# Grouped attentions: the rough pass for row maxima replaced by scores kept in SBUF and shifted by GpSimd and VectorE

## The chip, the cores and the metric

One Trainium2 chip, one of its cores. The metric is the device time of one execution in microseconds (us), the median of three runs. Engines: PE is TensorE (matmuls; PEld is its weight load, which runs beside it), ACT is ScalarE, DVE is VectorE, POOL is GpSimd, SP is the engine that issues most DMAs. SBUF is the on-chip memory, PSUM the eight accumulator banks that PE writes.

## The reference, cut to what matters

The program is a stack of four blocks, each a cross attention and a feed-forward part, over x of 4 x 256 tokens x 256 features, with a context of 4 x 1601 tokens. The change touches the second and the fourth attention, the "grouped" ones: 16 query heads share 4 key/value heads, head size 128. The fourth:

```python
q = rms_norm((hidden_states @ Wq).reshape(B, S, 16, 128), q_norm_w)
k = rms_norm((encoder_hidden_states @ Wk).reshape(B, 1601, 4, 128), k_norm_w)
v = (encoder_hidden_states @ Wv).reshape(B, 1601, 4, 128)
k, v = repeat(k, 4, axis=2), repeat(v, 4, axis=2)
scores = einsum("bqhd,bkhd->bhqk", q, k) / 128 ** 0.5
probs = softmax(scores, axis=-1)
out = einsum("bhqk,bkhd->bqhd", probs, v).reshape(B, S, 2048) @ Wo
```

The second is the same with a rotation by position (rope) of q and k, and with the 256 query tokens appended to the context, so 1857 keys. The softmax subtracts each query's largest score.

## The kernel before, in words

`grouped_attention` is called twice, as a1 (with rope) and a3 (without). A **group** is one batch and one key/value head: 16 groups. A group has 4 heads x 256 queries = 1024 query columns, taken in two halves of 512; half a group is called a **unit** here. Keys come in **tiles** of 128: KT = 15 with rope, 13 without. A **turn** is one key tile against 512 query columns, so a group is 30 or 26 turns. In each turn

- PE computes the scores (`scores`, L1125, L1127, L1129: three fp32r matmuls of 512 columns, high x high, high x low, low x high) with keys on the partitions, and then, for the turn before, the product with the values (`values`, L1140: four fp32 matmuls of 129 columns, the last column being the sum of the probabilities).
- ACT takes exp of the scores out of PSUM into `probs` (`exp`, L1252), and writes the negated row maxima, `negb`, into the PSUM bank in which the scores after next will accumulate (`seed`, L1262).

Since keys lie on partitions, the row maxima must be known before the scores are. So there is a **rough pass** (`R`): for each block of 128 queries PE computes high x high scores with the queries on the partitions (L1104, two times two matmuls: 1024 keys, and the rest), DVE reduces each half (L1483), takes the smaller of the two negated maxima (L1491), POOL multiplies the identity by it (L1324), and one matmul with ones (`NB`, L1112) spreads the 512 maxima of a unit over all partitions; DVE copies them to `negb` (L1498). That is 16 R tasks a group, 8 for the unit just ahead in the same group (R0 to R7) and 8 for the next group (R8 to R15).

Beside that each turn carries tasks for the next group: keys and values (`KV`, one a key tile), queries (`Q`), their norms on POOL (`KN`, `QN`), rope on DVE (`KR`, `QR`), transposes with a high/low split (`KX`, `QX`, `OX`), the output product (`Y`), weight splits (`W0` wkv, `W1` wq, `W2` wo) and, once a batch, the norm of x and the rope tables (`RA`). The table `GROUP_TURNS` says by hand in which turn each task stands; every engine runs its part of turn n in that order. The results of PE tasks go through two PSUM banks in turn: PE may start task i only when DVE has freed task i-2 (`begin`, `item_free`). Each weight has a staging buffer `wf` of its own. A block `_first` prepares group 0 (its list is `FIRST_TASKS`) and ends with R8 to R15; then `_groups` runs the 16 groups. x goes through copies in SBUF (`x_n`, `x_b`) that SP loads and stores.

## Time and profile before

| | |
|---|---|
| median of 3 runs | 3728.43 us (3725.1 to 3730.5) |
| span of the profiled execution | 3724.8 us |
| PE busy | 3484.8 us (94%) |
| PEld busy | 2986.2 us (80%) |
| DVE busy | 2317.7 us (62%) |
| ACT busy | 2244.6 us (60%) |
| POOL busy | 863.9 us (23%) |
| groups of a1 | 541.3 to 1753 us |
| groups of a3 | 2534.0 to about 3597 us |

Busy is the time in which the engine had an instruction in work. A matmul's duration holds its latency: two that follow one another start closer together than either lasts, so what a matmul costs PE is the distance between two starts in the timeline, not the mean of its group.

### The profile page before, as it was taken

To read this page: it belongs to the slowest core of one execution; us is meant where nothing else is said; L and a number is where in the kernel's file an instruction comes from. 1 tells how busy PE (TensorE), PEld (TensorE's weight loads), DVE (VectorE), ACT (ScalarE), POOL (GpSimd) and SP (SyncE) were. 2 spreads that over 40 slices of the span, in tenths; PEclk is the share of its full clock that TensorE was granted. 3 is DMA by queue.
4 is the path that set the end of the run, shared out by engine and by line. 5 is a ranking of instruction groups with operands and counts; after the bars stand their busy time and mean duration, and the time that the engine had idled before them with its cause. 6 is when DMAs were issued, how large, how long until landed. Compare 5 with 4: busy or idle time off the path is not lost. (4 is left out here: it accounts for less than half of the span.)

```text
span 3724.8 us, 63821 instructions
## 1 busy us (share of the span) xinstructions
PE 3484.8 (94%) x23912; PEld 2986.2 (80%) x23912; DVE 2317.7 (62%) x4551; ACT 2244.6 (60%) x5208; POOL 863.9 (23%) x1082
## 2 busy tenths in 40 slices
...
DMA packets 59186, 179.04 MB, mean 48 GB/s; under 512 B 6084, under 2 KB 27776, under 8 KB 53888
## 3 DMA queue, kind: packets, MB, share of 16 engines
q1 hardware_dynamic: 53024, 135.57, 10.6%
...
q14 instruction: 114, 0.93, 0.1%
...
## 5 line engine op out<-in xcount | busy, mean ns | idle before, releaser
L1140 PE MATMUL ps<-a_v_rows,a_probs 128*128 128x129 f32 (+1 forms) x7168 | 943.3, 276 | 0.5 <-DVE a_o_rows L1508 0.5
L1140 PEld LDWEIGHTS ps<-a_v_rows,a_probs 128*128 128x128 f32 (+1 forms) x7168 | 894.5, 191 | 41.1 <-issue 5.1
L1252 ACT ACTIVATE a_probs<-ps 128x512 f32<-128x512 f32 (+1 forms) x896 | 535.6, 598 | 606.0 <-PE ps L1129 604.8
L1483 DVE TENSOR_REDUCE a_neg<-ps 128x1 f32<-128x1024 f32 (+2 forms) x512 | 539.7, 1055 | 397.0 <-PE ps L1104 396.4
L1262 ACT ACTIVATE ps<-a_negb 128x512 f32<-128x512 f32 (+1 forms) x892 | 536.7, 602 | 58.3 <-DVE a_negb L1498 30.3
L1324 POOL TENSOR_SCALAR a_diag<-ident,a_negmax 128x128 fp32r<-128x128 f32 x256 | 157.1, 614 | 1466.1 <-DVE a_negmax L1491 1464.5
L1125 PE MATMUL ps<-a_qt,a_kt 128*128 128x512 f32 (+1 forms) x896 | 428.0, 478 | 1.4 <-PEq L72 1.4
L1031 PE MATMUL ps<-a_wr,a_ct 128*128 128x256 f32 (+1 forms) x2496 | 362.9, 287 | 19.0 <-DMA a_ct<-ctx_lo 16.9
L1031 PEld LDWEIGHTS ps<-a_wr,a_ct 128*128 128x128 f32 (+1 forms) x2496 | 336.4, 188 | 44.7 <-issue 15.7
L1129 PE MATMUL ps<-a_qt,a_kt 128*128 128x512 f32 (+1 forms) x896 | 354.9, 396 | 0.0
L1127 PE MATMUL ps<-a_qt,a_kt 128*128 128x512 f32 (+1 forms) x896 | 354.0, 395 | 0.0
L3331 ACT ACTIVATE a_probs<-ps 128x1024 f32<-128x1024 f32 x224 | 229.7, 1025 | 135.8 <-PE ps L3185 135.1
L1104 PE MATMUL ps<-a_kt,a_qt 128*128 128x512 f32 (+2 forms) x1024 | 292.6, 369 | 11.8 <-DVE a_negmax L1491 6.8
L3523 DVE TENSOR_REDUCE a_parts<-ps 128x1 f32<-128x448 f32 x384 | 222.0, 618 | 57.4 <-PE ps L3147 52.3
L1400 DVE TENSOR_TENSOR a_k_rows<-ps,a_kw 128x128 f32<-128x128 f32 (+1 forms) x448 | 128.8, 289 | 201.1 <-ACT a_v_rows L1219 188.6
L1104 PEld LDWEIGHTS ps<-a_kt,a_qt 128*128 128x128 f32 x1024 | 178.2, 192 | 68.5 <-DVE a_neg L1483 25.8
L1129 PEld LDWEIGHTS ps<-a_qt,a_kt 128*128 128x128 f32 (+1 forms) x896 | 165.6, 185 | 42.9
L1125 PEld LDWEIGHTS ps<-a_qt,a_kt 128*128 128x128 f32 (+1 forms) x896 | 169.9, 190 | 4.7 <-issue 2.8
L1127 PEld LDWEIGHTS ps<-a_qt,a_kt 128*128 128x128 f32 (+1 forms) x896 | 169.1, 189 | 0.8
L3185 PE MATMUL ps<-a_qt,a_kt 128*128 128x512 f32 x448 | 164.1, 448 | 2.5 <-ACT a_qt L3318 2.3
L3147 PE MATMUL ps<-a_kt,a_qt 128*128 128x448 f32 (+1 forms) x512 | 154.3, 368 | 5.0 <-ACT a_kt L3299 1.2
L1297 POOL TENSOR_TENSOR a_k_sq<-a_k_sq,nhalf 128x4 f32<-128x4 f32 (+2 forms) x128 | 151.0, 1180 | 10.7
...
## 6 DMA issues: line engine op xcount, KB each, us to landing
...
a_wf<-in_a_wkv SPq DMA_DIRECT2D x32, 256.0 KB, 2.7
...
```

The costliest lines, as they stand in the source:

```text
L1031: ins = pe.matmul(out[0:r, 0:2 * HD], src, wr[0][v][:, c * 2 * HD:(c + 1) * 2 * HD], start=(n == 0), stop=(n == 3 * DC - 1))
L1104: ins = pe.matmul(m.ps[:, rough_at(task) + k, 0:c1 - c0], queries[0][:, j * P:(j + 1) * P], keys[0][:, c0:c1], start=True, stop=True)
L1125: pe.matmul(out, kt[0][:, at:at + r], qt[0][:, cols], start=False, stop=False, skip_group_check=True)
L1127: pe.matmul(out, kt[0][:, at:at + r], qt[1][:, cols], start=False, stop=False, skip_group_check=True)
L1129: pe.matmul(out, kt[1][:, at:at + r], qt[0][:, cols], start=False, stop=True, skip_group_check=True).then_inc(st_ready, 1)
L1140: ins = pe.matmul(m.ps[:, 6 + i // 2, (i % 2) * 256:(i % 2) * 256 + VW], probs[0:r, n % 3, i * P:(i + 1) * P], v_rows[g % 2][0:r, t, :], s ...
L1252: act.activation(probs[0:r, n % 3, :], m.ps[0:r, 4 + n % 2, :], ACT.Exp)\
L1262: act.activation(m.ps[0:r, 4 + n % 2, :], negb[0:r, G, :], ACT.Copy).then_inc(seeded, 1)
L1483: ins = dve.tensor_reduce(neg2[:, j, r % 2:r % 2 + 1], flat2(m.ps[:, rough_at(task):rough_at(task) + 2, :])[:, 0:e - a0], AX.X, ALU.max, n ...
L3185: ins = pe.matmul(m.ps[:, 4 + 2 * (n % 2) + half, :], kt[g % 2][:, half, t * P:(t + 1) * P], qt[g % 2][:, half, :], start=True, stop=True)
L3331: act.activation(flat2(probs[n % 3][:, :, :]), flat2(m.ps[:, first:first + 2, :]), ACT.Exp)\
L3523: dve.tensor_reduce(to, slot(("R", h, j))[:, 0:n], AX.X, ALU.max, negate=True).then_inc(neg_done, 1)
```

## The change

1. **No rough pass.** `R` is gone from the tables and from PE, DVE and POOL. Scores start a fresh accumulation (`start=True`), in four banks (0, 1, 4, 5) in place of two.
2. **Scores are kept.** ACT copies each tile of scores to a slot of `ring` in SBUF (`keep`), KT + 5 slots deep. `seed` is gone.
3. **Maxima folded.** DVE takes the running maximum over the key tiles, `peak` (`highest`, once a turn but the first of a unit). At the end of a unit PE transposes it (`MX`, four transposes), DVE reduces it (one instruction), POOL makes the four diagonal blocks in one instruction, and `NB` spreads them as before.
4. **Shift later.** KT + 2 turns after the scores, `negb` is added in place to the slot: by DVE for key tiles 3, 7 and 11 of a unit, by POOL for the others (in the very last unit every second tile by DVE). A turn later ACT takes exp in place, in the same turn PE takes the product with the values, straight from the ring.
5. **Once, not twice.** Keys and queries of the next group (`kt`, `qt`) have one copy; one staging buffer `wf` serves all three weights, so each load waits for the split before it; x is read and written in place. The table of turns is new (its last two lines for a3 are shown), the queues run KT + 3 turns longer at the end, and `_first` has no R and no NB.

```diff
+    SHIFT_LAG, EXP_LAG, VALUE_LAG = KT + 2, KT + 3, KT + 3
+    RING = VALUE_LAG + 2
+    SCORE_BANKS = (0, 1, 4, 5)
 # GROUP_TURNS[False] (a3), turns 16 to 25
-        "R9 W0 Y0 R10 Y1", "R11", "R12", "R13", "R14 XC0", "R15 W2", "", "NB0 NX0", "",
+        "MX0 KN1", "NB0 KV8", "KV9 NZ0", "KV10", "OX1 KX0", "Y0 KV11", "Y1 KN2", "KX1 KV12 W2", "KN3", "W0 NX0", "",
+        "KX2", "KX3 QX1",
 # SP
-                        if ("W", g + 1, k) in splits:
-                            sp.wait_ge(w_lo, splits[("W", g, k)])
-                            load_weights(g + 1, k)
+                        i = splits[("W", g, k)]
+                        if i < len(weights):
+                            sp.wait_ge(w_lo, i)
+                            load_weights(*weights[i][1:])
 # PE
-                        for k, c0 in enumerate(range(a0, e0, 512)):
-                            c1 = min(c0 + 512, e0)
-                            ins = pe.matmul(m.ps[:, rough_at(task) + k, 0:c1 - c0], queries[0][:, j * P:(j + 1) * P],
-                                            keys[0][:, c0:c1], start=True, stop=True)
...
+                    def MX(g, i):
+
+                        out = begin(("MX", g, i))
+                        pe.wait_ge(peaked, peaks(KT * (unit_of(g, i) + 1) - 1))
+                        for j in range(JG):
+                            ins = pe.transpose(out[:, j * P:(j + 1) * P], peak[:, j * P:(j + 1) * P], m.ident[:, :])
+                        ins.then_inc(item_ready, 1)
...
+                        v = n - VALUE_LAG
+                        if attend and 0 <= v < TURNS:
+                            if v % KT == 1:
+                                values(v - 1)
+                            if v % KT:
+                                values(v)
 # ACT
-                        act.activation(probs[0:r, n % 3, :], m.ps[0:r, 4 + n % 2, :], ACT.Exp)\
-                           .then_inc(exp_done, 1)
...
-                        act.activation(m.ps[0:r, 4 + n % 2, :], negb[0:r, G, :], ACT.Copy).then_inc(seeded, 1)
+                        act.activation(slot(n)[0:r, :], m.ps[0:r, SCORE_BANKS[n % 4], :], ACT.Copy).then_inc(kept, 1)
+                    def exp(n):
...
+                        act.wait_ge(shifted_dve if by_turn[n] else shifted, shifts[by_turn[n]][n])
+                        act.activation(slot(n)[0:r, :], slot(n)[0:r, :], ACT.Exp).then_inc(exp_done, 1)
 # POOL
+                        pool.tensor_tensor(diag[:, :, :], m.ident[:, :].unsqueeze(1).to_broadcast([P, JG, P]),
+                                           negmax[:, u % 2, :].unsqueeze(2).to_broadcast([P, JG, P]), ALU.mult)\
...
+                        pool.tensor_tensor(slot(n)[0:r, :], slot(n)[0:r, :], negb[0:r, u % 2, :], ALU.add)\
+                            .then_inc(shifted, 1)
 # DVE
-                        ins = dve.tensor_reduce(neg2[:, j, r % 2:r % 2 + 1],
-                                                flat2(m.ps[:, rough_at(task):rough_at(task) + 2, :])[:, 0:e - a0],
-                                                AX.X, ALU.max, negate=True)
+                        dve.tensor_tensor(peak[0:r, :], (slot(n - 1) if t == 1 else peak)[0:r, :],
+                                          m.ps[0:r, SCORE_BANKS[n % 4], :], ALU.max).then_inc(peaked, 1)
+                        dve.tensor_reduce(negmax[:, unit_of(g, i) % 2, :].unsqueeze(2), src, AX.X, ALU.max, negate=True)\
...
+                        v, s = n - VALUE_LAG, n - SHIFT_LAG
+                        if attend and 0 < v < TURNS and v % KT == 0:
+                            outputs(v // KT - 1)
+                        if attend and n < TURNS and n % KT:
+                            highest(n)
+                        if attend and 0 <= s < TURNS and by_turn[s]:
+                            shift(s)
```

Two places in the order of instructions. The first is ACT in a1, around the split of W0 (`a_wr<-a_wf 128x512`, the next group's wkv). Before, in a full group:

```order
L1252 ACTIVATE a_probs<-ps 65x512
L1262 ACTIVATE ps<-a_negb 128x512
L1201 ACTIVATE a_wr<-a_wf 128x512
L1252 ACTIVATE a_probs<-ps 128x512
L1262 ACTIVATE ps<-a_negb 128x512
```

And now (L1266 is `keep`, L1272 is exp, `a_wr<-a_wf 128x1024` is the split of W2):

```order
L1250 ACTIVATE a_kt<-ps 128x512
L1213 ACTIVATE a_wr<-a_wf 128x1024
L1272 ACTIVATE a_ring<-a_ring 128x512
L1266 ACTIVATE a_ring<-ps 128x512
L1272 ACTIVATE a_ring<-a_ring 128x512
L1266 ACTIVATE a_ring<-ps 128x512
L1213 ACTIVATE a_wr<-a_wf 128x512
L1272 ACTIVATE a_ring<-a_ring 128x512
```

W0 now follows W2 by two turns and shares its staging buffer. An exp stands right behind it.

The second is DVE in a1, in the turns where the first rope products of keys and queries stand (`a_by_sin`, `a_by_cos`: products with the tables `a_cs`). Before:

```order
L1400 TENSOR_TENSOR a_k_rows<-ps,a_kw 128x128
L1413 TENSOR_TENSOR a_by_sin<-a_q_rows,a_cs 128x512
L1414 TENSOR_TENSOR a_by_cos<-a_q_rows,a_cs 128x512
L1400 TENSOR_TENSOR a_k_rows<-ps,a_kw 128x128
L1483 TENSOR_REDUCE a_neg<-ps 128x1
L1400 TENSOR_TENSOR a_k_rows<-ps,a_kw 128x128 x2
```

Now (L1499 is `highest`, L1524 the shift by DVE):

```order
L1499 TENSOR_TENSOR a_peak<-a_peak,ps 128x512
L1426 TENSOR_TENSOR a_k_rows<-ps,a_kw 128x128
L1439 TENSOR_TENSOR a_by_sin<-a_q_rows,a_cs 128x512
L1440 TENSOR_TENSOR a_by_cos<-a_q_rows,a_cs 128x512
L1499 TENSOR_TENSOR a_peak<-a_peak,ps 128x512
L1524 TENSOR_TENSOR a_ring<-a_ring,a_negb 128x512
L1426 TENSOR_TENSOR a_k_rows<-ps,a_kw 128x128
```

Every turn has a `highest` ahead of its tasks in place of a reduction every second turn, and the shift of a tile stands behind the `highest` of a much later one.

## Rows read from the trace of the kernel before

**Rows 1.** Windows: length; busy us of PE, PEld, DVE, ACT, POOL; granted clock; DMA.
```profile
1116.20:1423.90 307.70, 303.80 (x2091) 273.31 (x2090) 209.82 (x359) 210.76 (x534) 81.02 (x102) 0.99 0.09 31
2903.20:3306.20 403.00, 402.71 (x2789) 363.01 (x2788) 207.50 (x366) 271.49 (x711) 108.31 (x153) 1.00 0.12 38
```

**Rows 2.** Timeline of PE, a1: start us, duration us, engine, line, instruction.
```profile
1101.71 0.48 PE L1125 MATMUL ps<-a_qt,a_kt 128*128 128x512 f32 x1
1102.02 0.40 PE L1127 MATMUL ps<-a_qt,a_kt 128*128 128x512 f32 x1
1102.26 0.40 PE L1129 MATMUL ps<-a_qt,a_kt 128*128 128x512 f32 x1
1102.49 0.55 PE L1104 MATMUL ps<-a_kt,a_qt 128*128 128x512 f32 x2
1102.88 0.87 PE L1031 MATMUL ps<-a_wr,a_ct 128*128 128x256 f32 x6
1103.58 1.05 PE L1140 MATMUL ps<-a_v_rows,a_probs 128*128 128x129 f32 x8
1104.39 0.47 PE L1125 MATMUL ps<-a_qt,a_kt 128*128 128x512 f32 x1
...
1110.11 0.60 PE L1058 MATMUL ps<-ident,a_k_rows 128*128 128x128 f32 x4
1110.54 1.06 PE L1140 MATMUL ps<-a_v_rows,a_probs 128*128 128x129 f32 x8
```

**Rows 3.** Groups of instructions in a1, 620 to 1700 us: busy us, mean ns.
```profile
L1262 ACT ACTIVATE ps<-a_negb 128x512 f32<-128x512 f32 (+1 forms) x424 | 255.1, 602 | 29.3 <-DVE a_negb L1498 15.4
L1483 DVE TENSOR_REDUCE a_neg<-ps 128x1 f32<-128x833 f32 x227 | 254.8, 1122 | 176.7 <-PE ps L1104 176.5
L1252 ACT ACTIVATE a_probs<-ps 128x512 f32<-128x512 f32 (+1 forms) x424 | 253.7, 598 | 272.4 <-PE ps L1129 271.7
L1324 POOL TENSOR_SCALAR a_diag<-ident,a_negmax 128x128 fp32r<-128x128 f32 x114 | 70.3, 617 | 681.5 <-DVE a_negmax L1491 681.5
```

**Rows 4.** The same in a3, 2600 to 3500 us.
```profile
L1483 DVE TENSOR_REDUCE a_neg<-ps 128x1 f32<-128x1024 f32 x214 | 211.5, 988 | 163.4 <-PE ps L1104 163.3
```

**Rows 5.** POOL's instructions over the whole span, forms apart.
```profile
L1308 POOL TENSOR_TENSOR a_q_sq<-a_q_sq,nhalf 128x8 f32<-128x8 f32 x32 | 53.1, 1660 | 2.7
L2239 POOL TENSOR_TENSOR f_h<-f_full,f_h 128x512 fp32r<-128x512 f32 x24 | 31.0, 1292 | 54.8 <-ACT f_h L2211 54.8
```

**Rows 6.** Timelines in a1: DVE, then POOL over the same stretch, then ACT.
```profile
1093.09 0.69 DVE L1372 TENSOR_TENSOR a_ot<-ps,a_ot 128x512 fp32r<-128x512 f32 x1 [0.20 <-ACT a_ot L1244]
...
1097.46 0.68 DVE L1413 TENSOR_TENSOR a_by_sin<-a_q_rows,a_cs 128x512 f32<-128x512 f32 x1
1098.06 1.53 DVE L1414 TENSOR_TENSOR a_by_cos<-a_q_rows,a_cs 128x512 f32<-128x512 f32 x1
...
1109.02 1.23 DVE L1359 TENSOR_TENSOR a_wr<-a_wf,a_wr 128x1024 fp32r<-128x1024 f32 x1 [0.16 <-ACT a_wr L1201]
...
1093.16 1.05 POOL L1313 TENSOR_TENSOR a_q_rows<-a_q_rows,a_q_sq 128x512 f32<-128x512 f32 x1
...
1097.85 1.19 POOL L1301 TENSOR_TENSOR a_k_rows<-a_k_rows,a_k_sq 128x512 f32<-128x512 f32 x1
...
1120.82 1.06 ACT L1201 ACTIVATE a_wr<-a_wf 128x1024 fp32r<-128x1024 f32 x1
```

**Rows 7.** DMA issues of the page: KB each, us from issue to landing.
```profile
a_wf<-in_a_wkv SPq DMA_DIRECT2D x32, 256.0 KB, 2.7
```

**Rows 8.** Timelines at the end of both `_first` blocks.
```profile
527.09 0.69 DVE L1372 TENSOR_TENSOR a_qt<-ps,a_qt 128x512 fp32r<-128x512 f32 x1 [0.52 <-ACT a_qt L1240]
...
541.35 0.77 PE L1125 MATMUL ps<-a_qt,a_kt 128*128 128x512 f32 x1 [0.67 <-PEq L72]
...
2519.85 1.70 PE L1104 MATMUL ps<-a_kt,a_qt 128*128 128x512 f32 x4 [0.91 <-DVE a_kt L1372]
...
2533.99 0.77 PE L1125 MATMUL ps<-a_qt,a_kt 128*128 128x512 f32 x1 [0.72 <-PEq L72]
```

More of the change, by code:

```diff
@@ L1 @@
+import itertools
 from contextlib import ExitStack
@@ L770, in plan_groups @@
     turns = []
-    for g in range(GROUPS):
+    for g in range(GROUPS + 1):
         for names in GROUP_TURNS[rope]:
@@ L867, in run @@
             squared = [t for t in flat if t[0] == "KV"]
-            TURNS = len(turns) if attend else 0
-            ROUGH_DEEP = 1 if attend else 2
             norms = {(t[1] + 1 if attend else t[1]): t for t in flat if t[0] == "NX"}
@@ L1279, in _ @@
                                 does[task](g, i)
-                    for k in range(NG if attend else 0):
-                        act.wait_ge(end_turned, k + 1)
-                        act.activation(ot[0][:, k * 512:(k + 1) * 512], m.ps[:, 2 + k, :], ACT.Copy).then_inc(end_hi, 1)
+                        if attend and n == END_AT:
+                            end_high(0)
+                    if attend:
+                        end_high(1)
                 @block.gpsimd
@@ L1494, in NB @@
[L1494 to L1503 removed]
+                        x = m.x[:, (g - 1) // KVH * QT + q, :]
```

394 lines of the change are left out of this document (191 added, 203 removed), and 14 rows, old and new, of tables (FIRST_TASKS, GROUP_TURNS).

## The prediction

> **What bounds the kernel now.** Begin with the busy shares of the page: PE 94%, DVE 62%, ACT 60%, POOL 23%. Then take windows inside the two grouped attentions, cut from one copy of `negb` to the same copy four groups (a1) or six groups (a3) later [rows 1]. The reader should see two things: a group takes 307.7 / 4 = 76.9 us in a1 and 403.0 / 6 = 67.2 us in a3, and PE is busy in 98.7% and 99.9% of that at full clock (0.99, 1.00), while DVE stands at 68% and 51%, ACT at 68% and 67%, POOL at 26% and 27%. So PE sets the pace, and work taken from it is time, as long as no other engine makes it wait. What its work costs is read from distances between starts [rows 2]: a matmul of 512 columns 0.24, the three of a turn's scores 0.78 (1101.71 to 1102.49), the values of a tile 0.81 (1103.58 to 1104.39), a KV task 0.70, four transposes 0.43. Summing a whole group that way gives about 74.8 us of PE work in a1 and 65.8 in a3: some 2.1 and 1.4 us a group are waits already.
>
> **PE: the rough pass out, transposes in.** In a1 a block of queries costs PE 2 x 0.24 for the first 1024 keys and 0.39 for the rest (1102.49 to 1102.88) [rows 2], 0.87; eight blocks a group, 7.0 us. In a3 the rest is 577 columns, 0.27, so 0.74 x 8 = 5.9. MX adds 2 x 0.43 = 0.9 a group. NB stays. Net -6.1 and -5.0 us a group. One of 16 groups has half of its blocks in `_first`, so 15.5 groups: -94.5 and -77.5, together **-172 us**. All of it lies on the bounding engine.
>
> **The first blocks.** In a1 the last split before the rough pass ends at 527.8, and the groups begin at 541.35 [rows 8]. With one weight split and the change of blocks left, I allow 1.5 us: 12.1 saved. In a3 QX1 (transposes, a copy, a split, 2.7 us with the handovers) moves up to 2519.85 and 0.8 for the change of blocks follows: 2523.4 in place of 2534.0, 10.6 saved. **-23 us**, not covered by anything, since PE mostly waits there.
>
> **The other engines' sums, per group.** ACT trades the seed, 602 ns, for the copy to the ring; both forms are 512-column copies or exps of about 0.6 us [rows 3], so it keeps its 52.7 and 45.2 us [rows 1]: no bound. DVE loses 16 reductions (1122 ns in a1, 988 in a3 [rows 3, 4]) and their small minima, and gets a fold a turn but the first of a unit (28 and 24), two reductions of 512, and six shifts. The nearest row for the fold is the difference PSUM minus SBUF of 512 columns, 0.69, for the shift a product of two SBUF operands, 0.68 [rows 6]. a1: 52.4 - 18.0 - 1.3 + 30 x 0.69 + 6 x 0.68 = 58 us; a3: 34.6 - 15.8 + 26 x 0.69 + 4.1 = 41. POOL loses eight diagonals (0.617 [rows 3]), gets two large ones and 24 (a3: 20) shifts. Two rows bound a shift: 1.05 us for 512 columns with one operand broadcast [rows 6], and 1.29 with two full operands [rows 5]; the shift has two full ones, so 1.29. a1: 20.3 - 4.9 + 31.0 + 2.4 = 49 us; a3: 18.1 - 4.9 + 25.8 + 2.4 = 41. By sums alone nobody passes PE's 68.6 and 61.7. By waits it is another matter.
>
> **New waits.** I walked through a group by its turns, with the durations above.
> 1. *Maxima at the end of a unit* (two a group). After MX, PE has one set of values and one of scores before NB, 1.59 us. Reduction 0.69, diagonal 1.2 (between POOL's 1.05 and 1.29 for 512 columns) and three handovers of 0.15 (a score matmul lasts 0.40, the next starts after 0.24 [rows 2]) need 2.3. Stall 0.7 each, **1.4**.
> 2. *QN before the shift of tile 2.* POOL's power takes 1.66 [rows 5] and stands with the scaling of the rows (1.05) between two shifts. The exp and the values of tile 2 come about **0.8** late.
> 3. *W0 behind W2.* One staging buffer: W2's copy on ACT (1.06), its split on DVE (1.23 [rows 6]), the load of wkv (2.7 [rows 7]), then W0's copy on ACT, and behind that, in ACT's queue, the exp that the next values need. In a3, counted from the end of turn 20's scores: copy done at 3.0, split 4.25, data 6.95, W0's copy and the exp 8.4. PE wants that exp at 0.45 + 0.70 + 0.81 + 1.59 + 1.59 + 0.78 = 5.9. Stall **2.5** in a3, and 2.3 in a1, in the 14 groups that have a W0. Nothing covers it: four score banks let PE run ahead with scores, but the values stand in its queue.
> 4. *KN1 in a3* stands between the diagonal of MX0 and the shift of tile 12, needed two turns on: **0.9**.
> 5. *DVE in a1.* Here a behaviour of the two engines counts. POOL's scaling ran 1097.85 to 1099.04; a rope product on DVE, both operands in SBUF, issued at 1098.06, took 1.53 in place of 0.68, ending 0.55 after POOL did. A difference with one operand in PSUM (1093.09) took its plain 0.69 beside POOL's 1.05 at 1093.16 [rows 6]. So the fold is safe, but 24 rope products and sums, three weight splits and six shifts a group, 33 instructions, can be held by POOL, which after the change reads SBUF for some 39 us a group (24 x 1.29, six scalings, two diagonals), 52% of the time. Held for half of a POOL instruction, 0.6: 33 x 0.52 x 0.6 = 10 us. DVE then has 58 + 10 less the 1 there is already, 67 us, in 75. In turns 8 to 15, where QR, KR, folds and KV crowd, it falls behind PE; the two task banks absorb part. I take **2.4** us a group, between 0 (all absorbed) and 10 (none).
>
> The Trainium skill, "SBUF — State Buffer", section "Who interferes with whom", says that a VectorE instruction with two SBUF inputs and a GpSimd instruction that reads SBUF exclude each other for a whole instruction, and that one with at most one SBUF input is free. This rule speaks against the change in a1, where it adds both kinds; the trace agrees, by the 1.53 and the 0.69. Taken without it, wait 5 would vanish and the sum below would be 37 us less.
>
> New waits: a1 1.4 + 0.8 + 2.3 + 2.4 = 6.9, a3 1.4 + 0.8 + 2.5 + 0.9 = 5.6. The waits of today (2.1 and 1.4) mostly come from bunched KX and QX tasks, which the new table spreads; I let them go. A group: a1 76.9 - 6.1 + 4.8 = 75.6, a3 67.2 - 5.0 + 4.2 = 66.4.
>
> **The ends.** After the last scores of each attention the chain fold, MX, reduction, diagonal, NB, copy, shift, exp (about 8 us) has three tiles of values (2.4) as cover: +5 each. In the last group the turns are bare; a tile that DVE shifts behind its fold is ready 1.2 us late for a 1.59 us turn, three or four times: +4 each. In a1's first group PE has no values yet and DVE sets the pace: +4. Together +22. One staging buffer and the missing copies of x cost nothing else: the other loads have 8 turns or more.
>
> **The sum.** 15.5 x (-1.3) = -20 and 15.5 x (-0.8) = -12; two groups each without W0, -5 and -5; first blocks -23; ends +22: **-43 us**. Against the profile's own 3724.8 this is 3682; the median of the runs is 3.6 higher, so **3685**.
>
> **Rivals.** (a) *The waits overlap*: a PE held at W0 lets DVE and POOL catch up, so that half of the new waits count. Then 3.5 and 2.8 a group in place of 6.9 and 5.6: another -96, 3589. With none of them left, PE is the bound throughout: -172 - 23 + 8, 3541. For: DVE's and ACT's shares leave room in most turns. Against: W0's wait is a plain chain of four durations. (b) *Nothing gained*: all that PE saves is waited away, first blocks and ends cancelling: 3721 to 3736. (c) *Slower, VectorE and GpSimd exclude each other in a1*: POOL, running ahead through its shifts back to back, holds DVE for a full shift each time it holds it: 33 x 0.52 x 1.29 = 22 us, DVE 58 + 22, plus waits 1 and 2, 82.7 a group; +90 in a1 with -17 in a3, -23 and +22: 3800. It decides as soon as DVE is held for more than 76.9 - 58 = 19 us a group. For: 1.53 for 0.68. Against: POOL is idle for long stretches by its sum, and DVE's folds leave it free way.
>
> **How the numbers follow.** Forecast 3685 (own range 3640 to 3715): 0.45. Rival (a): 0.27. (b): 0.09. (c): 0.19, reaching from 3736 up. Leaving out a tenth at each side, the unknown 0 to 10 us of wait 5 included, gives 3600 to 3750. Faster by over 0.2% (7.5 us, about what a measurement of this kernel can tell from no change) is the forecast and (a), 0.72; within it 0.09; slower 0.19.
>
> **What would show it.** No rough matmuls (1024 before), 256 transposes of `peak`. Step 1: idle of PE at the ones matmul, ended by POOL's diagonal, 0.7 at a time. Step 3: ACT waiting for the DMA into `a_wf`, some 2 us, 28 times. Step 5: mean of the rope products above 1 us, DVE over 85% in a1. Windows over the same groups: 75.6 and 66.4. The prediction is wrong if POOL's shift lasts well over 1.29, if PE idles for exps that wait for a shift in every turn, or if the wait at W0 doesn't appear.

## The result, and the profile after

The changed kernel takes 3901 us (median; 3901 to 3903), the kernel before 3728 in the same session: ratio 1.046, 95% interval 1.045 to 1.048. The forecast was 3685 us, 3600 to 3750: wrong in its sign. The profiled execution has a span of 3901.4, against 3724.8.

First the page's busy times, then the windows over the same stretches as [rows 1] (from one copy of `negb` to the same copy four groups later in a1, six in a3; columns as there), then what PE waited for (total us, times, longest).

```profile
PE 3398.7 (87%) x23140; PEld 2878.9 (74%) x23140; DVE 2574.2 (66%) x4870; ACT 2187.7 (56%) x5212; POOL 1739.6 (45%) x1583
```
```profile
1205.30:1543.33 338.03, 295.33 (x1995) 261.19 (x1994) 255.85 (x406) 202.68 (x533) 205.83 (x174) 0.96 0.08 26
3059.95:3490.29 430.34, 384.27 (x2644) 340.61 (x2643) 236.32 (x413) 261.95 (x710) 256.16 (x237) 0.98 0.10 35
```
```profile
PE ps L1152 <- ACT a_ring L1272: 179.4, 171, 9.3
PE ps L1121 <- POOL a_diag L1337: 41.7, 64, 1.3
PE ps L1047 <- DVE a_k_rows L1426: 28.0, 22, 2.0
PE ps L1091 <- DVE a_o_rows L1533: 22.5, 31, 1.8
```

A group takes 338.03 / 4 = 84.5 us in a1 (76.9 in [rows 1]) and 430.34 / 6 = 71.7 in a3 (67.2). PE's busy time fell, by 303.80 - 295.33 = 8.5 in four groups and 18.4 in six (2.1 and 3.1 a group, where 6.1 and 5.0 were forecast; most of the difference is what it loses behind its waits, below). But what it no longer does it now waits, and more: its idle in these windows rose from 3.9 to 42.7 us and from 0.3 to 46.1. Most of it is values (L1152) waiting for an exp. No other engine is full: DVE 76% and 55%, POOL 61% and 60%. So the new bound isn't an engine but a chain of hand-overs.

Where in a group the time is lost, from PE's timeline, turn by turn. In a regular group (one without the next batch's work) the first score matmul comes 75.9 us after that of the group before in the old kernel and 81.5 in the new one (a1), 67.0 and 68.0 (a3). The idle of PE in it was 0.5 and 0.0; it is 8.7 and 5.1 (tiles are counted within a unit, from 0):

| wait of PE, us a group | a1 | a3 |
|---|---|---|
| ones matmul, for POOL's diagonal | 0.4 + 1.1 | 0.4 + 0.4 |
| values of tile 2, 3 (POOL's power ahead) | 0.9 + 0.2 | 0.9 + 0.2 |
| values of tile 7, first unit | **2.9** | **1.25** |
| values behind W2's copy on ACT | 0.6 | 0.5 |
| values of tile 12 (KN1) | - | 0.8 |
| KV task, for DVE's `k_rows` (turn 14) | 1.5 | - |
| OX0, for `o_rows` | 0.6 | 0.6 |
| values of two more tiles that DVE shifts | 0.6 | - |

The longest regular wait, in a1's group 8. PE, then DVE, POOL and ACT over the same stretch (start, duration, engine, line, instruction; in brackets the idle before it and who ended it):

```profile
1268.64 0.40 PE L1142 MATMUL ps<-a_qt,a_kt 128*128 128x512 f32 x1
1271.94 1.68 PE L1152 MATMUL ps<-a_v_rows,a_ring 128*128 128x129 f32 x8 [2.90 <-ACT a_ring L1272]
1273.27 0.78 PE L1140 MATMUL ps<-a_qt,a_kt 128*128 128x512 f32 x1
1273.84 0.63 PE L1141 MATMUL ps<-a_qt,a_kt 128*128 128x512 f32 x1
...
1266.94 1.05 DVE L1439 TENSOR_TENSOR a_by_sin<-a_k_rows,a_cs 128x384 f32<-128x384 f32 x1
1267.91 1.64 DVE L1440 TENSOR_TENSOR a_by_cos<-a_k_rows,a_cs 128x384 f32<-128x384 f32 x1
1269.58 0.69 DVE L1499 TENSOR_TENSOR a_peak<-a_peak,ps 128x512 f32<-128x512 f32 x1
1270.19 1.04 DVE L1524 TENSOR_TENSOR a_ring<-a_ring,a_negb 128x512 f32<-128x512 f32 x1
...
1264.04 9.66 POOL L1348 TENSOR_TENSOR a_ring<-a_ring,a_negb 128x512 f32<-128x512 f32 x6
...
1269.06 0.63 ACT L1213 ACTIVATE a_wr<-a_wf 128x512 fp32r<-128x512 f32 x1 [0.97 <-DMA a_wf<-in_a_wkv]
1271.26 0.63 ACT L1272 ACTIVATE a_ring<-a_ring 128x512 f32<-128x512 f32 x1 [1.57 <-DVE a_ring L1524]
```
```profile
1273.27:1276.50 3.23, 3.23 (x17) 2.84 (x17) 2.70 (x5) 1.31 (x3) 0.43 (x1) 0.60 0.28 62
```

Read it from the bottom. W0's copy does wait for its data (0.97, the forecast's wait 3), but it is over at 1269.7, and the exp behind it waits another 1.57 for DVE's shift. DVE is late because six shifts of POOL run back to back (9.66 us, 1.61 each), and beside them the two rope products of 384 columns take 1.05 and 1.64; the shift that follows takes 1.04 where 0.68 was reckoned. Then PE pays a second time. The turn of the wait, its idle taken off, took 2.27 where a turn without a wait takes 1.59, and the next turn ran at a granted clock of 0.60, the 1.2 GHz level for most of it: 3.23 us where the same turn costs 2.03 at 1.00. That second part does not always come. Twelve groups of a1 have this wait of 2.9, and in three of them (1, 3 and 14, counted from 0) the clock stayed at 1.00: the turn then took 1.85 net of its idle and the next one 2.02.

By shape, the rope instructions of before (first two rows) and after, and POOL's shift (count | busy us, mean ns):

```profile
L1414 DVE TENSOR_TENSOR a_by_cos<-a_k_rows,a_cs 128x384 f32<-128x384 f32 x16 | 8.8, 550 | 0.0
L1421 DVE TENSOR_TENSOR a_k_rows<-a_by_cos,a_by_sin 128x192 f32<-128x192 f32 x16 | 5.6, 350 | 0.0
```
```profile
L1440 DVE TENSOR_TENSOR a_by_cos<-a_k_rows,a_cs 128x384 f32<-128x384 f32 x16 | 21.8, 1366 | 0.0
L1447 DVE TENSOR_TENSOR a_k_rows<-a_by_cos,a_by_sin 128x192 f32<-128x192 f32 x16 | 21.8, 1361 | 0.0
L1348 POOL TENSOR_TENSOR a_ring<-a_ring,a_negb 128x512 f32<-128x512 f32 x633 | 891.5, 1432 | 21.5 <-DVE a_negb L1516 21.5
```

Once a batch there is more. In a3 PE waits 7.7 to 9.3 us for an exp: SyncE's queue issues the four loads of the next context just ahead of wkv's (SPq rows; SPq is SyncE's queue of DMA issues), and ACT waits for wkv with the exp behind it. In a1 the sine tables put 4.5 us on ACT ahead of an exp. The two groups around it take 87.4 and 87.8 us, a3's group 79 to 81.

```profile
3113.61 0.52 SPq L955 DMA_DIRECT2D a_ct<-ctx_hi  x1
...
3116.38 0.39 SPq L961 DMA_DIRECT2D a_wf<-in_a_wkv  x1
...
3125.58 0.63 ACT L1213 ACTIVATE a_wr<-a_wf 128x512 fp32r<-128x512 f32 x1 [7.43 <-DMA a_wf<-in_a_wkv]
```
```profile
1136.66 1.28 ACT L1277 ACT_TABLE_LOAD   x1
1137.96 1.90 ACT L1277 ACTIVATE a_cs<-a_cs 128x960 f32<-128x960 f32 x2
1139.87 1.28 ACT L1272 ACT_TABLE_LOAD   x1
```

### The profile page after: what moved, and what is told of

The parts are those of the page before. It is cut to its first block and busy times, and to the rows that moved or that the text cites. A ratio compares the mean times of both kernels' runs of the same rounds, so it can differ in the third digit from the quotient of the medians.

```text
span 3901.4 us, 63859 instructions
## 1 busy us (share of the span) xinstructions
PE 3398.7 (87%) x23140; PEld 2878.9 (74%) x23140; DVE 2574.2 (66%) x4870; ACT 2187.7 (56%) x5212; POOL 1739.6 (45%) x1583
## 3 DMA queue, kind: packets, MB, share of 16 engines
q0 software_dynamic: 3696, 37.68, 2.6%
## 5 line engine op out<-in xcount | busy, mean ns | idle before, releaser
L1152 PE MATMUL ps<-a_v_rows,a_ring 128*128 128x129 f32 (+1 forms) x7168 | 973.1, 281 | 181.9 <-ACT a_ring L1272 179.4
L1152 PEld LDWEIGHTS ps<-a_v_rows,a_ring 128*128 128x128 f32 (+1 forms) x7168 | 895.9, 195 | 250.7 <-ACT a_ring L1272 237.3
L1348 POOL TENSOR_TENSOR a_ring<-a_ring,a_negb 128x512 f32<-128x512 f32 (+1 forms) x697 | 983.7, 1436 | 21.5 <-DVE a_negb L1516 21.5
L1499 DVE TENSOR_TENSOR a_peak<-a_peak,ps 128x512 f32<-128x512 f32 (+1 forms) x768 | 526.7, 686 | 575.2 <-ACT a_ring L1266 556.8
L1266 ACT ACTIVATE a_ring<-ps 128x512 f32<-128x512 f32 (+1 forms) x896 | 531.4, 593 | 392.8 <-PE ps L1142 389.0
L1272 ACT ACTIVATE a_ring<-a_ring 128x512 f32<-128x512 f32 (+1 forms) x896 | 562.7, 630 | 285.5 <-DVE a_ring L1524 182.6
L1337 POOL TENSOR_TENSOR a_diag<-ident,a_negmax 128x512 fp32r<-128x512 f32 x64 | 70.8, 1105 | 457.7 <-DVE a_negmax L1505 457.7
L1229 ACT ACTIVATE a_square<-ps 128x128 f32<-128x128 f32 (+1 forms) x448 | 123.7, 276 | 164.2 <-PE ps L1047 137.0
L1311 POOL TENSOR_SCALAR a_k_sq<-a_k_sq 128x4 f32<-128x4 f32 (+2 forms) x128 | 28.9, 226 | 343.1 <-ACT a_v_rows L1233 339.7
L1524 DVE TENSOR_TENSOR a_ring<-a_ring,a_negb 128x512 f32<-128x512 f32 x199 | 160.1, 808 | 0.0
```

Source lines behind the costliest of these rows:

```text
L1152: ins = pe.matmul(m.ps[:, 6 + i // 2, (i % 2) * 256:(i % 2) * 256 + VW], slot(n)[0:r, i * P:(i + 1) * P], v_rows[u // NG % 2][0:r, t, :], ...
L1266: act.activation(slot(n)[0:r, :], m.ps[0:r, SCORE_BANKS[n % 4], :], ACT.Copy).then_inc(kept, 1)
L1272: act.activation(slot(n)[0:r, :], slot(n)[0:r, :], ACT.Exp).then_inc(exp_done, 1)
L1348: pool.tensor_tensor(slot(n)[0:r, :], slot(n)[0:r, :], negb[0:r, u % 2, :], ALU.add)\
L1499: dve.tensor_tensor(peak[0:r, :], (slot(n - 1) if t == 1 else peak)[0:r, :], m.ps[0:r, SCORE_BANKS[n % 4], :], ALU.max).then_inc(peaked, 1)
```

## The experiments

All of them at a glance. The last two columns are the mean of the same four groups of a1 and six of a3 as above, from the starts of their first score matmuls; ratios are to the kernel before, each with an interval of +-0.0018 at most.

| run | on top of | us | ratio | a1 | a3 |
|---|---|---|---|---|---|
| before | | 3728 | 1 | 76.9 | 67.2 |
| after | | 3901 | 1.046 | 84.5 | 71.7 |
| e1 wkv's own buffer | after | 3871 | 1.038 | 84.4 | 68.6 |
| e2 context load behind wkv | after | 3876 | 1.040 | 84.5 | 68.7 |
| e3 values a turn later | after | 3864 | 1.036 | 83.9 | 70.2 |
| e4 POOL shifts 32 columns | after | 3760 | 1.008 | 77.7 | 68.6 |
| e5 DVE shifts before fold | after | 3850 | 1.033 | 82.8 | 70.8 |
| e6 a3's shifts on DVE | e5 | 3834 | 1.028 | 83.6 | 69.5 |
| e7 POOL adds on a spare tile | before | 3830 | 1.027 | 81.5 | 69.0 |
| e8 all shifts on POOL | after | 3790 | 1.017 | 79.8 | 70.8 |
| e9 pass cut to 32 columns | before | 3560 | 0.954 | 71.7 | 62.7 |
| e10 e1 and e2 | e8 | 3743 | 1.003 | 79.2 | 67.0 |
| e11 values later, OX, Y moved | e10 | 3760 | 1.008 | 81.9 | 65.1 |
| e12 a3's shifts on DVE | e11 | 3792 | 1.016 | 82.0 | 67.2 |
| e13 one tile a group to POOL | after | 3853 | 1.033 | 81.4 | 71.7 |
| e14 e11's slack in a3 only | e10 | 3713 | 0.996 | 78.9 | 65.0 |
| e15 the power a turn ahead | e14 | **3696** | **0.992** | 78.1 | 64.9 |
| e16 KR2, KR3 three turns later | e15 | 3730 | 1.000 | 80.2 | 64.9 |

**e9: what is the pass worth?**

```
-  for k, c0 in enumerate(range(a0, e0, 512)):
-      c1 = min(c0 + 512, e0)
+  for k, c0 in enumerate([a0]):
+      c1 = c0 + 32            # and the reduction reads 32
```

> The kernel before (3728 us), leaving out work: each matmul pair of the rough pass has 32 columns in place of 1024 or the rest, and each reduction reads 32. It prices the forecast's largest term, the pass itself. In before's trace a turn that has nothing else takes 1.59 us without a block of the pass and 2.06 or 1.97 (a1), 2.06 or 1.94 (a3) with one: 0.43 and 0.41 a block, 16 blocks a group. With some 0.06 left of each: -5.9 and -5.6 us a group, 15.5 groups each: -178 us, 3550, if the time freed on TensorE is time. Rival (some other engine's chain is right behind TensorE): under 100 us gained, 3628 or more, with waits for exps in the bare turns.

Windows over the four and six groups:

```profile
1041.93:1328.77 286.84, 283.69 (x2029) 259.80 (x2027) 147.14 (x358) 209.26 (x534) 80.40 (x101) 0.99 0.10 33
2754.76:3130.85 376.09, 375.61 (x2693) 341.87 (x2692) 128.66 (x365) 270.52 (x710) 103.64 (x152) 1.00 0.12 41
```

-169 us against the same session's before, 9 short of expected; of it 153 lie between the first and the last scores of the two attentions (81 in a1, 72 in a3), where all 178 were expected, and the rest mostly in the blocks that prepare group 0. PE stays 99% busy, so nothing stood right behind it. The largest term of the forecast, the worth of the pass, holds in the main; the loss is in what was put in its place.

**e1 and e2: is it W0's load?** (the forecast's wait 3)

```
   # e1
+  wf0 = st.sb("wf0", [P, WIDTHS[0]])
...
-  return wf[:, 0:WIDTHS[k]]
+  return wf[:, 0:WIDTHS[k]] if k else wf0[:, :]
...            # SyncE: a load waits only for the split of its own buffer
   # e2, SyncE
-  for task, g, i in turn:
+  for task, g, i in sorted(turn, key=lambda t: t[0] != "W"):
```

> One change to the changed kernel (3901 us): wkv gets a staging buffer of its own, so that its load no longer waits for W2's split. Theory T, a sum of separate waits (waits 1 to 5 as forecast, and on top of each of them what the matmuls behind it lose, and waits that come once a batch): the wait of PE for the exp behind W0 goes. In a1 that is 2.9 us idle, 0.7 on the values behind it and 1.2 on the next turn at the lower clock, 4.8 in each of 14 groups, 67; in a3 1.25 + 0.27 in 11 groups, 17, and 12 in each of the three groups where the context is loaded, 36. Sum -120: 3781 us. Rival R, one engine's pace (VectorE and GpSimd holding each other set the time, and PE's waits only show where it falls due): PE waits elsewhere for what it no longer waits for here, and less than 40 us is gained: 3861 or more.

> One change to the changed kernel: where a turn has both W2 and KV12 (a3, turn 20, only there), SyncE's queue issues the load of wkv before the four loads of the next batch's context and not behind them. Theory T: the three waits of 7.7 to 9.3 us in a3 fall to the 1.25 of a regular group, and the six us at a lower clock behind each go: 12 us three times, -36: 3865 us; a1 stays as it is. Rival R: the wait moves to the next thing, under 10 us gained. If instead wkv's data come late because its packets share the queue with the context's, wkv first cures it as well, but the context's own readers would wait in its place.

PE and ACT in the same group of e1:

```profile
1275.67 1.74 PE L1155 MATMUL ps<-a_v_rows,a_ring 128*128 128x129 f32 x8 [2.89 <-ACT a_ring L1275]
...
1271.73 0.62 ACT L1216 ACTIVATE a_wr<-a_wf 128x512 fp32r<-128x512 f32 x1
1274.99 0.63 ACT L1275 ACTIVATE a_ring<-a_ring 128x512 f32<-128x512 f32 x1 [2.64 <-DVE a_ring L1527]
```

W0's copy no longer waits for data, and PE still waits 2.89 (2.90 before), with a3's 1.25 unchanged too. In both attentions DVE's shift of tile 7 ends later than W0's copy, and hides it. Group 14 of a1 in the changed kernel shows the same without any edit: it has no W0, and PE waits 2.90 in turn 25 all the same, for an exp that waits for DVE alone:

```profile
1771.29 0.63 ACT L1272 ACTIVATE a_ring<-a_ring 128x512 f32<-128x512 f32 x1 [3.18 <-DVE a_ring L1524]
```

With the shifts on POOL as well (e8, below) that wait of group 14 is gone. e1 gained 30 us where 120 were expected; its gain and e2's (25, of 36) are the same one, in the groups of a3 that load a context.

**e13, e5: the tile that ends last.**

```
   # e13
-  return t % 4 == 3
+  return t % 4 == 3 and not (rope and u % NG == 0 and t == 7)
   # e5, VectorE: the two calls change places
+  if attend and 0 <= s < TURNS and by_turn[s]: shift(s)
   if attend and n < TURNS and n % KT:          highest(n)
```

> One change to the changed kernel (3901 us): of the shifts of VectorE, those of tile 7 of a group's first unit in a1 (one a group, 16 in all) go to GpSimd. In the changed kernel that shift starts 2.6 us late behind two rope products of 1.0 and 1.6 us and the fold, PE waits 2.9 for its exp, the values behind it take 0.7 more and the next turn 1.2 more at the lower clock. Theory (this tile is the place where the exclusion meets PE): the wait falls to the 1.2 of e8 and the lower clock goes: 1.7 + 0.4 + 1.2 = 3.3 us in 14 groups of a1, -46: 3855 us, a regular group of a1 78.2 in place of 81.5. Rival (VectorE's share as a whole is too much for its queue in a1): the wait moves to tile 11 or to KX2, -10 or less.

> One change to the changed kernel (3901 us): on VectorE the shift of a tile stands ahead of the turn's fold, not behind it. Run e1 showed that the wait of PE at turn 23 of a3 (1.25) and turn 25 of a1 (2.9) is not W0's: both tiles are tiles 7, shifted by VectorE behind a fold that waits for the turn's own scores. Theory F (the fold ahead of it is the cause): in a3 that wait and the 0.27 behind it go, 1.5 in 16 groups, -24; in a1 turns 6, 10 and 29 (0.26, 0.19, 0.42, and 0.27 behind each) go and turn 25 keeps what the rope products ahead of it take, some 2.2: -2.3 in 16 groups, -37. Together 3840 us. Theory E (VectorE and GpSimd hold each other in a1, the fold only shows it): a3 gains its 24, a1 nothing or 10 us, since VectorE's queue is as long as before: 3870 to 3880.

One tile a group, 16 instructions in the whole kernel, is worth 3901 - 3853 = 48 us. In e13 PE's wait there is

```profile
1248.13 1.16 PE L1152 MATMUL ps<-a_v_rows,a_ring 128*128 128x129 f32 x8 [1.14 <-ACT a_ring L1272]
```

and the turn behind it is at full clock. A regular group of a1 fell from 81.5 to 78.4 us, of which 1.45 is idle (8.74 to 7.29); most of the rest is the clock, which no longer falls there.

In e5 the waits of 0.2 to 0.4 at DVE's other tiles went, but tile 7's stayed at 2.88 in a1 and 1.0 to 1.1 in a3: the fold was not what held it. DVE, POOL and PE in a1's group 5, then DVE and ACT in a3's group 7:

```profile
1001.82 1.64 DVE L1440 TENSOR_TENSOR a_by_cos<-a_k_rows,a_cs 128x384 f32<-128x384 f32 x1
1003.49 1.64 DVE L1524 TENSOR_TENSOR a_ring<-a_ring,a_negb 128x512 f32<-128x512 f32 x1
...
997.96 9.65 POOL L1348 TENSOR_TENSOR a_ring<-a_ring,a_negb 128x512 f32<-128x512 f32 x6
...
1005.84 1.16 PE L1152 MATMUL ps<-a_v_rows,a_ring 128*128 128x129 f32 x8 [2.88 <-ACT a_ring L1272]
```
```profile
3151.50 1.53 DVE L1524 TENSOR_TENSOR a_ring<-a_ring,a_negb 128x512 f32<-128x512 f32 x1
...
3153.56 0.63 ACT L1213 ACTIVATE a_wr<-a_wf 128x512 fp32r<-128x512 f32 x1 [0.76 <-DMA a_wf<-in_a_wkv]
3154.10 0.61 ACT L1272 ACTIVATE a_ring<-a_ring 128x512 f32<-128x512 f32 x1
```

In a1 the shift starts earlier but now lasts as long as one of POOL's, 1.64 for 1.04, and ends as late as before. In a3 it is held as well (1.53), though there is no rope, but there W0's copy now ends last. -52 us, between what the two theories gave, and a good part of it is neither's: this time the clock held behind 9 of the 12 waits of 2.88 (3 of 12 before the edit), as in the turn after the one shown:

```profile
1006.75:1008.80 2.05, 2.05 (x19) 1.86 (x17) 2.01 (x3) 1.10 (x4) 0.86 (x1) 1.00 0.03 8
```

A regular group of a1 so takes 78.4 in place of 81.5, with only 0.6 us less idle. Why the clock falls behind one wait of 2.9 us and not behind another is open.

**e8, e4, e7: VectorE's share, and the two engines' hold on each other.** (A hold: an instruction of one of the two lasts longer because one of the other is under way.) e8 and e4 change one line each, e7 adds one addition, on a tile of its own:

```
   # e8
-  by_turn = [by_vector(n) for n in range(TURNS)]
+  by_turn = [False for n in range(TURNS)]
   # e4, GpSimd
-  pool.tensor_tensor(slot(n)[0:r, :], slot(n)[0:r, :], negb[0:r, u % 2, :], ALU.add)
+  pool.tensor_tensor(slot(n)[0:r, 0:32], slot(n)[0:r, 0:32], negb[0:r, u % 2, 0:32], ALU.add)
   # e7, GpSimd in before, behind the turn's tasks
+  if attend and n % 4 != 3 and n < TURNS:
+      pool.wait_ge(st_ready, n + 1)
+      step(pool.tensor_tensor(spare[:, 0, :], spare[:, 0, :], spare[:, 1, :], ALU.add))
```

> The changed kernel with VectorE's share of the shifts given to GpSimd, so that every tile is shifted by GpSimd (1.44 us each, 6 to 7 more a group). Theory F: the tiles that stood behind a fold are ready early, which is worth what e5 is worth, about -40 to -60, and GpSimd has 60 us of work in a group of 80 (a1) and 50 in 66 (a3). Theory E: in a1 GpSimd's shifts run back to back through turns 22 to 29 (1.6 each there against turns of 1.59), it falls behind and holds VectorE for longer: a1 gets slower by 1 to 4 us a group, a3 faster by 1: 3890 to 3930.

> Leaves out work: GpSimd adds the maxima to 32 of a tile's 512 columns only; its order, its waits and VectorE's shifts stay. It takes some 1.2 us of GpSimd's 1.44 off each of 697 shifts, and with them what they hold VectorE up. Theory T: the wait for k_rows in a1 (1.5 to 1.7) and the waits behind the power and the scalings (0.9, 0.26, 0.84) shrink; W0's, the two at the maxima and the batch ones stay: about 3 us a group with what stands behind them, -60 to -90, 3810 to 3840 us. Rival R (GpSimd's time and the exclusion between the two engines are what costs): most of PE's waits for exps go, W0's too, -170 or more: 3730 or less.

> The kernel before (3728 us), with one thing added in the two grouped attentions: after the scores of three turns in four GpSimd adds 512 columns to 512 others in SBUF, on a spare tile that nobody reads, 22.5 times a group in a1 and 19.5 in a3, behind the turn's tasks in its queue. Nobody waits for them, except GpSimd's own later tasks. Theory E (a VectorE instruction with two operands in SBUF and a GpSimd instruction hold each other): rope products and sums in a1 grow from 0.7 and 0.4 to above 1 us, GpSimd's add from 1.29 to 1.4 or more, and a1, whose PE has 0.5 us of idle a group, gets slower by 1 to 4 us a group, a3 by less than 0.5: +20 to +60. If the contention were harmless: +5 or less, and rope products as before.

e7, groups by shape:

```profile
L1354 POOL TENSOR_TENSOR a_spare<-a_spare 128x512 f32<-128x512 f32 x672 | 906.6, 1349 | 199.6 <-PE ps L1130 185.9
L1418 DVE TENSOR_TENSOR a_by_sin<-a_k_rows,a_cs 128x512 f32<-128x512 f32 x48 | 49.2, 1025 | 5.6 <-POOL a_k_rows L1302 5.6
L1418 DVE TENSOR_TENSOR a_by_sin<-a_k_rows,a_cs 128x384 f32<-128x384 f32 x16 | 18.3, 1145 | 0.1
```

Adds on a tile that nobody reads cost the old kernel 102 us: 4.6 a group in a1, 1.8 in a3. The product of 512 columns over the keys grew from 0.70 to 1.03, that of 384 from 0.55 to 1.15. In a regular group of a1 PE now waits for DVE at four places (0.2 to 0.9 each) and 1.1 for POOL's diagonal; in a3, where there is no rope, it waits for POOL's scaling of the rows, queued behind the adds (0.3 and 0.8 in one group, 1.7 and 0.7 in the next). So both are shown, the hold in a1 and plain queueing in a3, and either costs without any new dependence. The Trainium skill, "SBUF — State Buffer", section "Who interferes with whom", adds that the order of issue decides which of the two is blocked. The rows agree with a hold in both directions, since DVE's product of 384 columns went from 0.55 to 1.37, and POOL's shift took 1.28 alone (1217.12) and 1.61 in the run of six above.

e4 shows the same from the other side: with POOL's shift at 0.33 us the product of 384 columns is back at 0.55 and the sum of 192 at 0.36, PE's wait for `k_rows` (1.5) and at tile 2 (0.9) are gone, tile 7 waits 1.2: -142 us, nearer to the rival's 170 than to the theory's 60 to 90. The wait of 1.1 at the ones matmul of turn 16 stays, so the hold is not its cause. (e4 leaves most of the shift out, so it takes away POOL's time as well as the hold, and doesn't tell the two apart.)

```profile
L1440 DVE TENSOR_TENSOR a_by_cos<-a_k_rows,a_cs 128x384 f32<-128x384 f32 x16 | 8.8, 549 | 0.0
```

e8 was off most: -111, where the two theories had -40 to -60 and -10 to +30. The rope products are as slow as before (1.36 for 384 columns), and POOL is busier (74% in a1), yet little that PE needs now stands in DVE's queue behind them: the wait for `k_rows` is 0.9, tile 7's is 1.2, and the clock stays at 1.00 in the regular groups (76.3 us in place of 81.5, with 3.1 less idle). The hold as such is not the harm; it is the harm on a path that ends at PE.

**e3, e11, e14: slack.** 

```
-  SHIFT_LAG, EXP_LAG, VALUE_LAG = KT + 2, KT + 3, KT + 3
-  RING = VALUE_LAG + 2
+  SHIFT_LAG, EXP_LAG, VALUE_LAG = KT + 2, KT + 3, KT + 4
+  RING = VALUE_LAG + 1
   # e11, a1 turns 4, 5 and 19 to 23 (a3 likewise)
-  "W1 OX0 ...", "KV0 ...", ... "OX1 KX0 KR4", "Y0 KR5 KV13", "Y1 KV14", "KX1 KN3 W2", "KR6 N0"
+  "W1 ...", "OX0 KV0 ...", ... "KX0 KR4", "OX1 KR5 KV13", "Y0 KV14", "Y1 KX1 KN3", "W2 KR6 N0"
   # e14
+  VALUE_LAG = KT + (3 if rope else 4)        # and the moved tasks in a3's table alone
```

> One change to the changed kernel: the values of a tile come one turn later (VALUE_LAG + 1, ring of the same size), so that an exp may be up to 1.6 us late without PE waiting for it. Theory T: the waits for an exp of under 1.6 us go with the 0.27 that each costs behind it. A group of a1 waits 2.4 us in turns 5, 6, 10, 23 and 29, and 2.9 behind W0, of which 1.3 stays: -2.4 - 1.35 - 1.6 - 0.7 = -6; a3 has 0.9, 0.2, 0.8, 0.5 and 1.25: -3.7 - 1.35 = -5. 16 groups each: -176, and a few us back because the drain has a tile more: 3730 us. Rival R: the pace is VectorE's and GpSimd's, a turn of slack is used up within a group and the waits come back: 3860 or more.

> The kernel of e8 (all shifts on GpSimd, 3790 us) with e1's buffer for wkv and e2's order of the loads. In e8 PE still waits 1.2 (a1, turn 25) and 1.1 (a3, turn 23) for the exp behind W0's copy, and 7.7 in the three groups of a3 that load the context. In e1 the same step gained nothing in a1 because VectorE's shift of the tile stood behind it; here there is none. If the waits of that tile are separate causes in one place, uncovering them one by one pays: 1.5 us in 14 groups of each attention, -41, and -9 three times, -27: 3720 us. If W0 is again not what PE waits for: -27 only, 3762.

> The kernel of e10 with e3's turn of slack for the values, and OX and Y (with W2) moved one turn down the table, since in e3 the waits for o_rows, a_ot and x_slots grew to 2.1 us a group when only the values were moved. Theory: the waits for exps behind the power and behind W2's copy (a1 0.9, 0.6; a3 0.9, 0.8, 0.5, with 0.27 behind each, and the 3.5 behind the sine tables half) go, and about 1.2 a group comes back at turn 0, where PE reaches the next unit before KX3 and QX1 are split: -1 us a group in a1, -2 in a3, -6 at the tables: e10 - 50, about 3670. Rival (the slack is eaten up, as in e3): e10 - 10 or less.

> The kernel of e10 (3743 us) with the turn of slack for the values and the moved tasks of e11 in a3 alone; a1 stays as in e10. If the two attentions are independent, a1 keeps its 75.5 a group and a3 takes 64.5: 16 x 1.9 = 30 us less than e10: 3712 us, under the kernel before's 3729.

In e3 the waits for exps went nearly as expected (regular groups of a3: none left), and others came in their place: OX for `o_rows`, Y for DVE's addition, the next unit for the last key block (1.7 in a1), so that the idle of a group went from 5.1 to 4.5 and from 8.7 to 8.9: -38 of -171. e10 (-47 against e8) lies between its two cases: uncovering W0 now paid 0.9 a group in a3's regular groups, 0.8 in a1's, and in a3's batches the rest. e11 moved the tasks as well: a3 gained its 1.9 a group, a1 lost 2.7, with PE waiting for DVE's splits of `ot` and for the fold (1.2 and 1.5). There DVE is the engine with no slack, and values that come later only press its tasks together. e14 takes the one and leaves the other: 3713, expected 3712.

**e6, e12: a3's shifts on VectorE.**

```
   # e6, in by_vector (VectorE's shift ahead of its fold, as in e5)
+  if not rope: return True
   # e12 (VectorE's shift ahead of its fold here too)
+  by_turn = [not rope for n in range(TURNS)]
```

> The kernel of e5 with one more change, in a3 alone: VectorE shifts every tile, GpSimd none. VectorE then has about 41 - 4 + 26 x 0.69 = 55 us of work in a group of 65, GpSimd some 12. Theory E/T: the waits behind GpSimd's power and scalings (turns 5, 6 and 15: 0.9, 0.2, 0.8, with 0.27 behind each) go, and nothing holds VectorE: a group of a3 64 us in place of 66.5, -40 us against e5. Against it: 55 of 64 is a queue that is full in the turns with KV, KX and W; if VectorE's order is what makes PE wait, a group stays at 66 or more and nothing is gained.

> The kernel of e11, with the shifts of a3 on VectorE, ahead of the fold, and those of a1 on GpSimd. No shift then runs beside rope work on the other engine's account in a3, and a1 keeps VectorE free. e6 against e5 gave -1.1 us a group of a3 for this. Expected: e11 - 10 to - 20, about 3655. If VectorE, at 55 us of 64, falls behind now that PE waits less: the same as e11 or slower by up to 20.

e6 gained 1.3 a group of a3, 16 us in all of 40. Its a1, the same instructions as e5's with the same idle, took 83.6 in place of 82.8, since the clock fell behind turn 25 in 8 of its 12 groups with a wait of 2.9, and in 3 of e5's: 11 us over the whole of a1 in the two profiled executions. On the tuned table of e11 the same edit loses 2.1 a group (65.1 to 67.2, +31 us). POOL's waits go, but PE waits for DVE at the split of `ot` (1.1) and of the last key block (0.9). DVE is busy for 304.59 of 402.96 us there, 76%: not full, but no longer early where it matters.

**e15, e16: two of the forecast's places by themselves.** e15 splits QN0 into its power (QP0) and its scaling; e16 moves KR2 and KR3.

```
   # e15, a1 turns 3 and 4 (a3 likewise)
-  "QN0 RA6", "W1 OX0 RA7 PR0 GP4"
+  "QP0 RA6", "W1 OX0 RA7 PR0 QN0 GP4"
...
   # e16, a1 turns 14 to 18
-  "QX0 KV9 KR2 ...", "MX0 KR3 ...", "NB0 KV10 ...", "KV11 ...", "KN2 KV12"
+  "QX0 KV9 ...", "MX0 ...", "NB0 KV10 ...", "KR2 KV11 ...", "KR3 KN2 KV12"
```

> The kernel of e14, with GpSimd's power for the queries (1.7 us) in turn 3 and the scaling that follows it (1.05) a turn later, so that one shift stands between them. Forecast's wait 2: the shift of tile 2 stands behind both, PE waits 0.9 (turn 5 of a1, 1.2 in e10) and loses 0.27 behind it. It goes: -1.2 to -1.5 in 16 groups of a1; a3 has the slack already and gains nothing: e14 - 20, about 3692. If the wait comes from something else in that turn, nothing.

> The kernel of e15, with the rope products and sums of keys 4 to 7 (KR2, KR3) in turns 17 and 18 of a1 in place of 14 and 15. Forecast's wait 5 put VectorE's backlog at turns 8 to 15: PE waits 0.8 to 1.0 for k_rows in turn 14 and 1.0 at the ones matmul in turn 16. If rope work in front of them is the cause, both shrink to 0 and 0.4: -1.5 in 16 groups, e15 - 24. If the backlog only moves on (GpSimd shifts in turns 17 and 18 too), 0 to +10.

e15: 3696, expected 3692; PE's wait at tile 2 is gone. This kernel is faster than the one before and the changed one; its ratio to the one before is 0.992 (0.990 to 0.993). Its windows:

```profile
1064.94:1377.22 312.28, 287.25 (x1996) 254.71 (x1995) 244.46 (x382) 202.95 (x535) 236.95 (x197) 0.99 0.09 28
2847.71:3236.83 389.12, 374.87 (x2646) 334.40 (x2644) 210.49 (x378) 261.69 (x711) 292.81 (x272) 1.00 0.12 38
```

e16 was expected at -24 and is +33. The wait at the ones matmul of turn 16 fell from 0.99 to 0.40 as thought, so rope work was in its way; `k_rows` in turn 14 stayed at 0.8; and a new wait of 2.15 stands in turn 19 (behind it the clock fell in groups 1, 5, 9 and 13, which cost 1.6 each):

```profile
1219.51 1.48 DVE L1452 TENSOR_TENSOR a_k_rows<-a_by_cos,a_by_sin 128x256 f32<-128x256 f32 x1
1221.03 0.28 DVE L1431 TENSOR_TENSOR a_k_rows<-ps,a_kw 65x128 f32<-65x128 f32 x1
...
1219.27 2.86 POOL L1353 TENSOR_TENSOR a_ring<-a_ring,a_negb 128x512 f32<-128x512 f32 x2
...
1221.37 0.66 PE L1077 MATMUL ps<-ident,a_k_rows 128*128 128x128 f32 x4 [2.15 <-DVE a_k_rows L1431]
```

A sum of 256 columns, 0.42 alone, takes 1.48 beside two shifts, with a task bank's release behind it.

## Why the prediction was wrong

What failed is the forecast's balance of waits: new ones of 6.9 us a group in a1 and 5.6 in a3, less 2.1 and 1.4 of "the waits of today", against 6.1 and 5.0 of work saved. The runs show 8.7 and 5.1 of waits, next to nothing let go (0.5 and 0.0), about 2.9 and 1.4 more that PE loses behind its waits, and 59 us of once-a-batch waits, none of which the sum had. By its own steps, for a regular group unless said otherwise:

- **The pass** (-172 with MX in): right in the main. e9 puts the pass, but for 32 columns a block, at -169, 153 of it in the groups, where -178 was expected; so the term may be up to 25 us too large.
- **First blocks** (-23): -7 and -8, so -15. Right in kind.
- **Wait 1, maxima** (1.4 a group): 1.5 in a1, 0.8 in a3. Twice 0.4 is what the chain itself costs, half of the forecast; the 0.7 more at turn 16 of a1 is rope work in VectorE's queue, as e16 shows (0.99 to 0.40), so that the agreement in a1 is luck.
- **Wait 2, QN** (0.8): 0.9, with 0.2 in the next turn. Right, and shown by e15.
- **Wait 3, W0** (2.5 in a3 and 2.3 in a1): wrong, and this is where the walk through the turns went astray. The chain of four durations exists (ACT waits for wkv's data 28 times, but mostly 0.8 to 1.1 us), and alone it costs 1.1 and 1.2 (e8), half of the forecast; but at the same tile a later one ends: DVE's shift. The forecast had even named that lateness ("a tile that DVE shifts behind its fold is ready 1.2 us late"), but charged it to the last group only. 2.9 in a1 is what the rope work ahead of it and POOL's shifts beside it make of it (1.2 with POOL's shift cut to 32 columns, e4). e1 shows that W0 cost nothing there as long as this stood.
- **Wait 4, KN1** (0.9): 0.8. Right.
- **Wait 5, DVE in a1** (2.4 in turns 8 to 15): 1.5 in turn 14, and 0.7 of turn 16, right in size; but the other half of the same mechanism was overlooked, turns 22 to 25, where two weight splits, rope work and a shift that PE needs stand in one queue. With turn 25 (2.9) that makes 5.1, a good deal more than 2.4.
- **"The waits of today, let go"** (-2.1 and -1.4): they weren't there. PE's idle before was 0.5 and 0.0. In a1 1.0 of it lies in the 76.9 itself, a mean that has the batch's work in it (a regular group takes 75.9); the rest is that the summed durations came out too low, and the difference was called a wait. Some 3.0 us over both, 16 groups: +48. The profile said it: 98.7% and 99.9% busy [rows 1].
- **What PE loses behind a wait**: not in the forecast. Each wait at a value matmul cost another 0.27 (its turn 2.57 in place of 2.30 net of the idle), six times a group in a1 and five in a3; and behind the 2.9 us the clock went to its lower level in 9 of the 12 groups of a1 that have it, 1.6 each. Together 2.9 a group in a1, 1.4 in a3, +68. How often it falls isn't settled by a1's own instructions: they are the same in e5 and e6, and it fell in a different share of the groups.
- **Once a batch**: not in the forecast, though the table shows it. The context's loads ahead of wkv (three times 11 to 12 us), the sine tables and z in a1 (25 over three batches): +59.
- **Ends** (+22): +32, with the first group counted in (the end of each attention, less the 0.81 of each tile whose values have only moved there from the first group).

These misses add up: 48 + 68 + 59, the waits that were larger than taken (+29 in a1, -8 in a3), +10 at the ends, +8 at the first blocks: 214, for a difference of 220 between -43 and the +177 of the two profiled executions (the rest of the program gave back 5, so that some 11 us are not accounted for). Rival (c) had the right sign and 82.7 a group of a1 (84.5 measured), with a3 mistaken; its mechanism is shown by e7 and, at the one tile, by e13; e4 agrees. But its condition, DVE held for more than 19 us a group, was not met (DVE's busy time is 64 a group, not 80): PE doesn't wait for the sum of DVE's work, it waits at the two or three places where a held instruction stands before one it needs. That is why the sums, the 45% given to the forecast and the 19% given to (c), all looked at the wrong quantity.

A check of the list as a whole is e15: with all shifts off DVE's queue, wkv's own buffer and order, a turn of slack in a3 and the power a turn ahead, the kernel is 205 us faster than the changed one (3901 to 3696). It lands near the forecast's 3685 by other means, for some of these edits also remove waits that the forecast had counted in, while others stay.

Open is why `k_rows` in turn 14 stays late in e16, when the clock falls behind a wait of 2.9 us, and how much of the 102 us of e7 is the hold alone: in a1 the adds also delay POOL's own scalings.
